# A decoder layer with 4-bit attention weights: a second block of Q's projection from exact codes, scaled inside the PSUM bank by ScalarE

## The reference

```
q = h @ dequant(q_codes, q_scales)   # h = layernorm(x); K and V alike
dequant: (codes - 8) * repeat(scales, 128, axis=0)   # 4-bit codes, one scale per 128 rows and column
q, k = rope(q), rope(k)              # 32 Q heads, 8 K/V heads, head size 128
out = softmax(q k^T / sqrt(128) + causal mask) v     # per head and batch
x = x + out @ dequant(o_codes, o_scales)
x = x + fake_quant(layernorm(x)) @ fake_quant(ctx)
x = x + layernorm(x) @ binarize(ffn_weight)^T
```

## Time and profile before

| | us |
|---|---|
| median of 3 runs | 1073.74 (1073.23 to 1074.12) |
| the profiled execution | 1073.24 |
| its span, first to last instruction | 1071.4 |
| 60 of the 64 slots, from the first exact block to the last | 194 to 887 |

### The profile page before, as it was taken

One profiled execution on the slowest core, in us unless ns is written; L12 is line 12 of the kernel. 1 busy time (PEld: TensorE's weight loads), 2 busy tenths in 40 slices (PEclk: granted clock), 3 DMA queues, 4 the chain that ended last, 5 costly groups with the idle time before them and its releaser, 6 DMA issues.

```text
span 1071.4 us, 18946 instructions
## 1 busy us (share of the span) xinstructions
PE 1030.9 (96%) x5356; PEld 505.7 (47%) x5356; DVE 935.7 (87%) x1741; ACT 706.3 (66%) x1557; POOL 768.7 (72%) x817
## 2 busy tenths in 40 slices
PE   5999998999999999999999999999999998989998
PEld 3444443444555455455545554544544453444443
DVE  7988998799888888888888889999999999878873
ACT  5547757777777777777777777767776776463320
POOL 4678887888778787777878778988988898332100
PEclk9999999999999999999999999999999999999999
DMA  9774303679767766766776666777777666423543
GB/s 341 245 191 129 112 22 80 148 153 162 163 164 152 162 154 160 150 163 159 155 152 158 161 147 153 157 148 155 165 158 149 151 127 130 114 91 64 99 104 78
DMA packets 309827, 156.13 MB, mean 146 GB/s; under 512 B 257728, under 2 KB 270400, under 8 KB 309728
## 3 DMA queue, kind: packets, MB, share of 16 engines
q1 hardware_dynamic: 301952, 141.69, 57.9%
q10 hardware_dynamic: 7776, 13.37, 4.5%
HBM read 89.20 MB, written 4.19 MB: 87 GB/s over the span
## 4 chain that ended last, share of the span: by engine, by line
PE 38%; POOL 35%; issue 11%; DVE 9%; ACT 5%; DMA 1%; ACTq 0%; POOLq 0%; DVEq 0%; SPq 0%
POOL w_b L1647 10%; POOL prob L1640 8%; POOL swapped L1635 5%; PE proj_ps L1107 5%; POOL q_sb L1660 3%; PE side_ps L929 3%; PE proj_ps L949 3%; PE out_ps L949 3%; PE side_ps L743 3%; PE side_ps L745 3%; PE side_ps L744 3%; POOL rot L1655 3%; PE proj_ps L1112 2%; PE score_ps L1078 2%; DVE rot L2007 2%
## 5 line engine op out<-in xcount | busy, mean ns | idle before, releaser
L1647 POOL TENSOR_TENSOR w_b<-prob,w_b 128x896 f16<-128x896 f32 (+2 forms) x192 | 188.3, 995 | 62.5 <-ACT w_b L1327 62.3
L1640 POOL TENSOR_SCALAR prob<-prob,row_inv 128x512 f32<-128x512 f32 (+3 forms) x256 | 177.9, 705 | 61.9 <-DVE row_inv L2180 59.0
L1300 ACT ACTIVATE prob<-score_ps,neg_max 128x512 f32<-128x512 f32 (+3 forms) x256 | 132.5, 520 | 78.3 <-DVE neg_max L2078 74.6
L743 PE MATMUL side_ps<-hT,w_a 128*128 128x512 f16 x444 | 168.3, 379 | 0.0
L744 PE MATMUL side_ps<-hT,w_a 128*128 128x512 f16 x444 | 168.3, 379 | 0.0
L745 PE MATMUL side_ps<-hT,w_a 128*128 128x512 f16 x444 | 168.3, 379 | 0.0
L2102 DVE SCALAR_TENSOR_TENSOR x_acc<-out_ps,o_now,x_acc 128x1024 f32<-128x1024 f32 x120 | 153.2, 1277 | 0.0
L2102 DVE SCALAR_TENSOR_TENSOR x_acc<-proj_ps,o_now,x_acc 128x1024 f32<-128x1024 f32 x120 | 152.8, 1273 | 0.0
L949 PE MATMUL proj_ps<-work,w_b 128*128 128x512 f16 x496 | 127.3, 379 | 4.3 <-issue 2.3
L949 PE MATMUL out_ps<-work,w_b 128*128 128x512 f16 x496 | 127.3, 379 | 0.9 <-DVE x_acc L2102 0.8
L2078 DVE CUSTOM_DVE_ANT_0 score_ps<-score_ps,mask_b 128x512 f32<-128x512 f32 (+3 forms) x256 | 122.2, 498 | 1.9 <-PE score_ps L912 0.9
(11 more groups left out here) (269 smaller groups left out, 2169.0 us busy)
## 6 DMA issues: line engine op xcount, KB each, us to landing
stage_c<-in_codes_dram SPq DMA_DIRECT2D x72, 256.0 KB, 2.8
stage_o<-in_codes_dram SPq DMA_DIRECT2D x64, 256.0 KB, 2.9
stage_s<-in_scales_dram SPq DMA_DIRECT2D x64, 256.0 KB, 3.4
...
```

The lines of the kernel that those rows point to most:

```text
L743: pe.matmul(o, stat(0), mov(0), start=first, stop=False)
L1300: ins = act.activation(prob[:, SCORE_AT[qb]:SCORE_AT[qb] + w], score_ps[:, score_bank(i, u), off:off + w], ACT.Exp, bias=neg_max[:, c:c + ...
L1640: return pool.tensor_scalar(prob[:, at:at + w], prob[:, at:at + w], row_inv[:, col:col + 1], P_UP, ALU.mult, ALU.mult)
L1647: ins = pool.tensor_tensor(prob16[:, 1, to:to + w], prob[:, at:at + w], prob16[:, 0, to:to + w], ALU.subtract)
```

## The change

Blocks 0 and 1 both go by exact codes, and in Q's own bank. `q_exact(0)` puts block 0 into `q_ps`; ScalarE scales the bank in place by the ratio of block 0's scale to block 1's; `q_exact(1)` adds block 1 onto it; ScalarE scales the bank by block 1's scale; blocks 2 to 7 are added onto that. `q_join` is gone; ScalarE copies the finished bank to `q_sum_in` (`q_copy`), which frees it for the next Q. The exchange of halves stays on ScalarE but stands between the two splits, ahead of the eviction of the weighted sum, which goes to the slot's end. In a head's first piece, 256 instead of 128 columns need no scales, so that the loads, `piece_scale` and `piece_lo` of these are shorter. The table has two columns, the ratio (guarded against a scale of zero) and block 1's scale, made in seven K tiles (4 to 10). The order inside the lists changes as the diff shows. Left out of it: names, shapes, the flag that lets a group of matmuls start on a bank with something in it, and which V blocks stand where in slot 2 (12 to 15 behind the first scores, 15 to 16 behind the second).

```diff
 Q_AHEAD = 2
-EXACT = P
-EARLY = 2
+N_EXACT = 2
+EXACT = N_EXACT * P
 Q_LEAD = 3
...
                     sp.wait_ge(piece_done, p + FIRST_PIECES)
-                    load_piece(q_index(*after), (i + 1) % 2)
+                    load_piece(q_index(*after), (i + 1) % 2, (0, EXACT)[i % B])
...
-            def q_exact(g, i):
+            def q_exact(g, i, e):
                 h = i // B
                 p = g * SLOTS + i
-                pe.wait_ge(piece_done, g * SLOTS + (2 * h + 2))
-                pe.wait_ge(ao_ready, p - 3)
+                if e:
+                    pe.wait_ge(q_based, 2 * (p - FIRST_PIECES) + 1)
+                else:
+                    pe.wait_ge(piece_done, g * SLOTS + (2 * h + 2))
+                    if known(p) and p == FIRST_PIECES:
+                        pe.wait_ge(q_summed, 3)
+                    else:
+                        pe.wait_ge(q_copied, p - FIRST_PIECES)
+                w = (h % RING * KB + e) * P
                 for l in range(2):
-                    mm = pe.matmul(pv_ps, w_a[:, 0, h % RING * KB * P:(h % RING * KB + 1) * P],
-                                   hT[:, l, 0, i % B * S:(i % B + 1) * S], start=l == 0, stop=l == 1)
+                    mm = pe.matmul(q_ps, w_a[:, 0, w:w + P], hT[:, l, e, i % B * S:(i % B + 1) * S],
+                                   start=l + e == 0, stop=l == 1, skip_group_check=e > 0)
                 mm.then_inc(q_exact_done, 1)
             def q_part(g, i, kbs):
                 h, b = divmod(i, B)
                 p = g * SLOTS + i
-                first = 1 if by_parts(p) else 0
+                first = N_EXACT if by_parts(p) else 0
                 if known(p) and p < Q_AHEAD and kbs[0] % 4 == 0:
...
                         pe.wait_ge(o_table_ready, 1)
-                    elif known(p) and p <= FIRST_PIECES:
-                        pe.wait_ge(q_summed, (1, 1, 3)[p - 2])
+                    elif known(p) and p < FIRST_PIECES:
+                        pe.wait_ge(q_summed, 1)
                     else:
-                        pe.wait_ge(q_joined, p - FIRST_PIECES)
+                        pe.wait_ge(q_based, 2 * (p - FIRST_PIECES) + 2)
                 for kb in kbs:
                     mm = three_products(q_bank(p), lambda l: w_a[:, l, (h % RING * KB + kb) * P:(h % RING * KB + kb + 1) * P],
-                                        lambda l: hT[:, l, kb, b * S:(b + 1) * S], kb == first, kb == KB - 1)
+                                        lambda l: hT[:, l, kb, b * S:(b + 1) * S],
+                                        kb == first and not by_parts(p), kb == KB - 1, by_parts(p))
                 if kbs[-1] == KB - 1:
...
                     pe.wait_ge(ao_ready, p)
-                if not (known(p) and (p == 0 or p >= N_SLOTS - FIRST_PIECES + 1)):
-                    pe.wait_ge(q_based, p)
...
                     v_blocks(v_at[1], v_at[2])
+                parts = by_parts(p + Q_AHEAD)
+                if has_ahead and parts:
+                    q_exact(*ahead, 0)
                 if has_o and not (known(p) and p == O_LAG):
                     o_unit(p - 1, prev[1], 3)
                 scores(p, i, g, 1)
+                if has_ahead and parts:
+                    q_exact(*ahead, 1)
                 if v_at:
                     v_blocks(v_at[2], v_at[3])
-                parts = by_parts(p + Q_AHEAD)
-                if has_ahead and parts:
-                    q_part(*ahead, range(1, EARLY))
                 if has_o:
                     o_unit(p, i, 0)
-                if has_ahead and parts:
-                    q_exact(*ahead)
-                elif has_ahead:
+                if has_ahead and not parts:
                     q_part(*ahead, range(0, 1))
-                if has_ahead and parts:
-                    q_part(*ahead, range(EARLY, 3))
                 scores(p, i, g, 2)
...
                     v_blocks(v_at[3], v_at[4])
+                if has_ahead:
+                    q_part(*ahead, range(N_EXACT if parts else 3, KB))
                 if has_o:
                     o_unit(p, i, 1)
-                if has_ahead:
-                    q_part(*ahead, range(3, KB))
-                if has_o:
                     o_unit(p, i, 2)
...
                 if by_parts(p):
-                    act.wait_ge(q_joined, p - FIRST_PIECES + 1)
+                    act.wait_ge(q_copied, p - FIRST_PIECES + 1)
                 swap(q_swap_of(p), q_sum_in if by_parts(p) else q_bank(p), q_swapped)
-            def q_base(g, i):
+            def q_copy(p):
+
+                act.wait_ge(q_done, p + 1)
+                act.activation(q_sum_in, q_bank(p), ACT.Copy).then_inc(q_copied, 1)
+
+            def q_base(g, i, e):
                 p = g * SLOTS + i
-                act.wait_ge(q_exact_done, p - FIRST_PIECES + 1)
-                if not (known(p) and p == FIRST_PIECES):
-                    act.wait_ge(q_cosed, p)
+                act.wait_ge(q_exact_done, 2 * (p - FIRST_PIECES) + (e + 1))
                 if known(p) and p < Q_LEAD * B:
-                    act.wait_ge(o_table_ready, 2)
+                    act.wait_ge(q_ratio_step, RATIO_STEPS)
                 else:
                     act.wait_ge(o_now_ready, g * RF + (i // B - (Q_LEAD - 1)))
-                act.activation(q_sum_in, pv_ps, ACT.Copy, scale=o_now[:, (i // B + 1) % 2, CB:CB + 1])\
+                act.activation(q_ps, q_ps, ACT.Copy, scale=o_now[:, (i // B + 1) % 2, CB + e:CB + e + 1])\
                     .then_inc(q_based, 1)
...
+                next_q = (g, i + Q_AHEAD) if i < SLOTS - Q_AHEAD else (g + 1, i + Q_AHEAD - SLOTS)
                 if with_ctx:
...
                     act.dma_start(ctx_raw[:, :], tile.rearrange("a p n -> (a p) n")).then_inc(ctx_landed, 16)
+                if has_ahead and by_parts(p + Q_AHEAD):
+                    q_base(*next_q, 0)
                 if known(p) and p == 1:
...
                 exps(p, i, 0)
+                if has_ahead and by_parts(p + Q_AHEAD):
+                    q_base(*next_q, 1)
                 if has_next and not by_parts(p + 1):
                     q_hi(p + 1)
+                o_cut(p, i)
                 exps(p, i, 1)
-                if has_ahead and by_parts(p + Q_AHEAD):
-                    q_base(*((g, i + Q_AHEAD) if i < SLOTS - Q_AHEAD else (g + 1, i + Q_AHEAD - SLOTS)))
                 if known(p) and wf_late(p) is not None:
                     wf_upper(wf_late(p))
+                exps(p, i, 2)
                 if with_ctx:
                     act.wait_ge(ctx_landed, q * 16 + 16)
                     act.activation(ctx_codes, ctx_raw[:, :], ACT.Identity, scale=scal[:, 5:6],
                                    bias=scal[:, 3:4]).then_inc(ctx_scaled, 1)
-                exps(p, i, 2)
                 if has_next and by_parts(p + 1):
                     q_hi(p + 1)
-                if has_piece:
-                    q_cut(p, i)
                 if with_ctx:
                     act.wait_ge(ctx_scaled, q + 1)
                     act.activation(dst, ctx_codes, ACT.Copy, bias=-Q_MID).then_inc(ctx_free, 1)
+                if has_piece:
+                    q_cut(p, i)
                 if known(p) and 0 < p < O_LAG:
                     v_evict(V_HERE + p - 1)
                 if known(p) and wf_early(p) is not None:
                     wf_sign(wf_early(p))
-                o_cut(p, i)
+                if has_ahead and by_parts(p + Q_AHEAD):
+                    q_copy(p + Q_AHEAD)
+                elif has_ahead:
+                    q_swap(p + Q_AHEAD)
+                if has_prev and known(p) and p < O_LAG:
+                    ao_part(p - 1, i - 1)
                 prob_split(p, 0)
-                if has_prev and not (known(p) and p == N_SLOTS - 1):
+                if has_ahead and by_parts(p + Q_AHEAD):
+                    q_swap(p + Q_AHEAD)
+                prob_split(p, 1)
+                if known(p) and p == N_SLOTS - 1:
+                    column_part(0, 0)
+                if not (known(p) and p < O_LAG):
                     ao_part(p - 1, (i - 1) % SLOTS)
-                if has_ahead:
-                    q_swap(p + Q_AHEAD)
-                if known(p) and p == N_SLOTS - 1:
-                    prob_split(p, 1)
-                    column_part(0, 0)
-                    ao_part(p - 1, i - 1)
-                    return
-                prob_split(p, 1)
+
             def q_first(n):
...
-                pool.wait_ge(q_joined, p - FIRST_PIECES + 1)
+                pool.wait_ge(q_copied, p - FIRST_PIECES + 1)
                 pool.wait_ge(q_ready, p)
...
                     if not (known(p) and p >= N_SLOTS - 1) and by_parts(p + 1):
+                        q_turn(p + 1)
                         sine(swapped[:, :], q_swapped, p + 1, q_sined)
-                        q_turn(p + 1)
                     if known(p) and wf_early(p) is not None:
...
-            def q_join(p):
-
-                dve.wait_ge(q_done, p + 1)
```

(48 more changed lines are left out.)

32 lines of the change are left out of this document (19 added, 13 removed).

## The result

The changed kernel takes 1065.59 us, median of four runs (1065.44 to 1067.70), beside 1073.63 us for the kernel before: ratio 0.9929, 95% interval 0.9917 to 0.9941. That is faster, by 8.0 us where 16.0 were forecast, and 0.1 us beyond the upper end of the range.

What follows compares the result with a forecast made beforehand. TensorE, with no idle time in the attention slots, was taken as the bound; -12.95 - 2.7 + 0.3 + 1.0 + 0.3 - 2.0 = -16.05 us gave 1057.7 us, range 1054.0 to 1065.5.

Steps and rivals of the forecast that it cites:

- The matmul and its price: TensorE, Q's blocks: 22 matmuls instead of 23 for 60 pairs at 0.216 us each, 12.95 us less; slot period 11.46 us.
- 2.7 us of stalls: Slots with dense weights and first eight slots: without the join VectorE no longer delays TensorE's O unit, -2.7 us.
- The two new waits: TensorE ahead of blocks 1 and 2: ScalarE's scalings finish with 0.6 and 0.14 us to spare, so 0 us.
- The first rival: Ahead of block 2: TensorE waits for the second scaling because exps(0) is late, 1081.7 us; chance 0.09.
- ScalarE in a context slot: Two more ScalarE instructions per context slot: 10.18 of 11.46 us busy, 89%; it fits, though the queue is in order.
- The loop's edges: Three loop turns: VectorE's late start delays exps(0) and the second scaling, some 0.7 us per edge, +0.3 us for three.
- The ratio table: Seven K tiles: eleven small VectorE instructions for three, 0.9 us more work, a third of it counted, +0.3 us.
- The first slots: Slots 0 to 2: exchange ahead of first split delays slot 1's transposes, which a weighted sum needs, +1.0 us.
- The last slots: Last two slots, bound by VectorE: slot 62 starts without lag, POOL and q_hi some 2 us earlier, -2.0 us.

Runs made afterwards that it cites:

- The best order tried: Changed kernel, ScalarE's loop written out, ratio steps between K additions, both splits ahead of eviction in slots 2 and 3, wf_sign ahead of Q's bank copy: 1055.96 us.
- the failed one: Changed kernel, ScalarE's loop written out, ratio steps between K additions, both splits ahead of eviction in slots 2 and 3, wf_sign between them: 1058.36 us.

## Why the prediction was right and wrong

- **The matmul and its price: right.** Every plain slot from 4 to 61 is 11.46 or 11.47 us, and the stalls without context are gone; -15.71 us against -15.22. The forecast counted 2.7 us of stalls; the slots of the kernel before hold 3.2.
- **The two new waits: right in the steady slots.** The scaling inside the bank took 0.66 us where 0.69 was taken, with 0.80 as the upper end, and block 2 does not wait. The first rival did not occur there: exps(0) starts at most 2.75 us into a plain slot (2.67 to 2.75 in the slots with the dense weights), and the rival began at 2.85. There the margin is 0.1 us, thin enough to call it luck in part.
- **ScalarE in a context slot: right in its result, thin in its margin.** 89% busy in the plain slots, as forecast, but the room is that of a ring with VectorE, about 0.5 us, which the prediction did not follow round.
- **The loop's edges: the step that failed most, 4.0 of the 8.3 us.** The prediction says that block 1 waits for ScalarE's own turn, but gives that no price. It took the rows of one edge, where the bracket names VectorE, and followed VectorE's 1.73 us through a chain to block 2: 0.7 per edge. The limit was ScalarE's turn, 2.93 to 3.13 us of idle time, straight in front of the scaling that the change put first in the slot: 2.1 per edge. The rows of before held the warning: ScalarE began 4.49, 4.44 and 4.66 us into the edge slots, and block 1 is wanted at 2.59. With ScalarE's loop written out the loss is gone; with VectorE's it stays.
- **The ratio table: mis-sized.** 0.20 us per step, +0.3 in sum; about 1.5 us were lost by steps that ended with GpSimd's instruction, and moving the steps gave them back. The row taken as the nearest had no GpSimd instruction beside it, and the rule of the Trainium skill cited above, which speaks against that price for some forms, was not weighed.
- **The first slots: mis-sized and misplaced.** +1.0 was put on the transposes of slot 1, which the weighted sum in slot 2 needs. They did start later, 2.2 instead of 0.2 us into slot 2, but of that slot's 0.97 us more only 0.31 are a wait for them:

```profile
201.38 1.80 PE L941 MATMUL side_ps<-work,v_sb 128*128 128x512 f16 x12 [0.31 <-DMA work<-w_b]
```

The larger loss was in slot 3, to which the prediction gave nothing: ScalarE's queue with 2.27 us and the clock with 1.69. The best order tried took back 1.6 us of slots 3 to 5 against the failed one; what holds the rest stays open.
- **The last slots: right in size, by another path**, -1.9 against -2.0. The prediction said that the transposes would still bind the weighted sum of slot 62, and that the last slot's maximum would follow its scores within 1 us. The wait for the transposes fell from 1.57 to 0.14 us and one for VectorE's O addition grew from 0.67 to 1.26; the maximum still comes 2.54 us behind the scores. That the sum agrees is in part luck.
